# Self-attention scores as pairs of 64-row matmuls into two banks, and one input's statistics behind the softmax of a step

## The reference

```python
q = (xp @ Wq + bq)            # 16 heads of 32 features
k = (xp @ Wk + bk)            # 2 groups of 32 features
v = (xp @ Wv + bv)
starts = jnp.arange(num_windows) * (W // 2)      # W = 64
idx = starts[:, None] + jnp.arange(W)
scores = jnp.einsum('brgnqd,bgnkd->brgnqk', qg, kw) * scale
attn = jax.nn.softmax(scores, axis=-1)
og = jnp.einsum('brgnqk,bgnkd->brgnqd', attn, vw)
x = x + (o @ Wo + bo)
```

## Time and profile before

| what | value |
|---|---|
| median of 3 runs | 2509.7 us (2509.41 to 2511.34) |
| profiled execution | 2509.38 us |
| its span, first to last instruction | 2507.7 us |
| TensorE busy | 2419.8 us (96%) |
| weight loads busy | 2203.8 us (88%) |
| VectorE busy | 1680.1 us (67%) |
| ScalarE busy | 1302.3 us (52%) |
| GpSimd busy | 1169.9 us (47%) |
| windows 179 to 229 us, one turn | TensorE 48.81, VectorE 39.93, ScalarE 36.83, GpSimd 37.77 us busy, granted clock 1.00 |
| window 34 to 42 us, in turn 0 | TensorE 6.64 of 8.00 us busy, granted clock 0.79 |

### The profile page before, as it was taken

One profiled execution on the slowest core, in us unless ns is written; L12 is line 12 of the kernel. 1 busy time (PEld: TensorE's weight loads), 2 busy tenths in 40 slices (PEclk: granted clock), 3 DMA queues, 4 the chain that ended last, 5 costly groups with the idle time before them and its releaser, 6 DMA issues. The chain is left out here.

```text
span 2507.7 us, 45795 instructions
## 1 busy us (share of the span) xinstructions
PE 2419.8 (96%) x14893; PEld 2203.8 (88%) x14893; DVE 1680.1 (67%) x4774; ACT 1302.3 (52%) x3307; POOL 1169.9 (47%) x1561
## 2 busy tenths in 40 slices
PE   7999998899999999999999999999999999999798
PEld 6998998789989998999898889999999999999686
DVE  7877887566565756565666666675757575767676
ACT  6777776455454545454554545454545454545511
POOL 6767776344343435343433434343435353435254
PEclk9999999999999999999999999999999999999899
DMA  4445456211111211211222211111111111122343
GB/s 143 159 148 172 168 167 218 104 46 58 44 54 54 65 40 54 58 44 54 61 92 60 84 35 59 44 54 54 55 47 61 43 55 54 44 73 95 126 145 121
DMA packets 101476, 207.69 MB, mean 83 GB/s; under 512 B 20048, under 2 KB 49456, under 8 KB 101152
## 3 DMA queue, kind: packets, MB, share of 16 engines
q1 hardware_dynamic: 95680, 186.78, 23.2%
q0 software_dynamic: 5600, 18.41, 2.2%
HBM read 139.83 MB, written 65.32 MB: 82 GB/s over the span
## 5 line engine op out<-in xcount | busy, mean ns | idle before, releaser
L1436 POOL TENSOR_SCALAR x_probs<-x_probs,x_inv 112x376 f32<-112x376 f32 x512 | 634.6, 1250 | 190.7 <-DVE x_inv L1636 190.7
L1430 POOL TENSOR_SCALAR x_bias<-x_top 112x1 f32<-112x1 f32 x512 | 124.1, 242 | 878.4 <-DVE x_top L1608 878.0
L1492 ACT ACTIVATE x_probs<-x_probs,x_bias 112x376 f32<-112x376 f32 x512 | 308.4, 603 | 421.0 <-POOL x_bias L1430 421.0
L1751 PE MATMUL x_ps_r<-x_wo,x_oT 128*128 128x512 f32 x1344 | 344.4, 392 | 1.4 <-DVE x_wo L1534 1.4
L1697 PEld LDWEIGHTS x_ps_o<-x_pT,x_v 128*128 128x128 f32 (+1 forms) x2304 | 294.2, 191 | 35.9 <-DVE x_pT L1615 17.5
L1737 PE MATMUL x_ps_f<-x_xT,x_wq 128*128 128x448 f32 x1440 | 319.2, 371 | 2.6 <-DVE x_v L1579 2.0
L1697 PE MATMUL x_ps_s<-x_kT,x_qT 128*112 128x376 f32 x1536 | 311.6, 338 | 3.5 <-DVE x_top L1608 3.4
L1697 PE MATMUL x_ps_f<-x_wv,ctxT 128*128 128x512 f32 (+1 forms) x1152 | 305.7, 403 | 8.0 <-DVE x_kT L1579 4.8
L1697 PE MATMUL x_ps_o<-x_pT,x_v 128*128 128x224 f32 (+1 forms) x2304 | 299.3, 274 | 11.8 <-DVE x_pT L1615 11.7
L1697 PE MATMUL x_ps_f<-ctxT,x_wk 128*128 128x376 f32 x1512 | 300.3, 334 | 2.1 <-DVE x_kT L1579 2.1
L1737 PEld LDWEIGHTS x_ps_f<-x_xT,x_wq 128*128 128x128 f32 x1440 | 262.6, 188 | 28.7 <-DVE x_v L1579 8.7
(11 more groups left out here) (236 smaller groups left out, 4000.3 us busy)
## 6 DMA issues: line engine op xcount, KB each, us to landing
ctxT<-ctxs SPq DMA_DIRECT2D x62, 752.0 KB, 4.5
ctxs<-ctxT SPq DMA_DIRECT2D x32, 752.0 KB, 5.0
x_xT<-h2T SPq DMA_DIRECT2D x15, 896.0 KB, 4.9
room<-in_ctx_dram SPq DMA_DIRECT2D x32, 256.0 KB
experts<-in_L_ffn_W_dram SPq DMA_DIRECT2D x32, 256.0 KB, 4.6
w_xa<-in_x_dram SPq DMA_DIRECT2D x32, 224.0 KB, 4.7
w_xr<-in_x_dram SPq DMA_DIRECT2D x32, 224.0 KB, 4.2
x<-w_xr SPq DMA_DIRECT2D x32, 224.0 KB, 5.1
```

The costliest lines, as they stand in the source:

```text
L1430: pool.tensor_scalar(bias[:, m:m + 1], top[:, m:m + 1], -0.1 * NEG, -SCALE, ALU.max, ALU.mult) \
L1436: pool.tensor_scalar(probs[0:T, m, 0:SE], probs[0:T, m, 0:SE], inv[:, m:m + 1], None, ALU.mult).then_inc(normed, 1)
L1492: act.activation(probs[0:T, m, 0:SE], probs[0:T, m, 0:SE], ACT.Exp, bias=bias[:, m:m + 1], scale=SCALE, accum_out=total[:, m:m + 1]).then_ ...
L1751: last = pe.matmul(ps_r[:], oT[:, a, h, slot:slot + P], wo[:, b_, h, :], start=h == 0 and (a, b_) == PASSES[0], stop=h == H - 1 and (a, b_ ...
```

## The change

The scores of a chunk are computed by halves of the rows. For each of the six products of a chunk there are two matmuls, one with rows 0 to 63 and one with rows 64 to 127, and each has only the 128 columns of `kd` in which these rows have values. The lower half writes bank `ps_s[0]`, the upper half `ps_s[1]`. A step then has 48 matmuls of 64 rows by 112 by 128 columns in place of 24 of 128 rows by 112 by 256 columns. Both banks are complete at the end of the block. The heads of a bank come in another order, and the product with the values reads `pT` in that order.

There is one wait for the banks at the start of a block in place of one per bank, and in step 0 a wait per chunk for the Q fill in place of one per two chunks.

Input 2 of the next turn moves from early to late in step 1 (`AHEAD`): its statistics on VectorE stand between the two `totals`, its `factors1` on GpSimd behind `normalise`. ScalarE's `norm1` of it moves to step 2, ahead of `exps` (`NORM_NEXT`). This holds for turns 0 to 6.

```diff
-    AHEAD = [([0], [1]), ([2], []), ([3], []), ([], [])]
+    AHEAD = [([0], [1]), ([], [2]), ([3], []), ([], [])]
+    NORM_NEXT = {1: [2]}
...
+                    ahead = fills.which(turn) in ("first", "full")
+                    if ahead:
+                        for n in NORM_NEXT.get(s - 1, []):
+                            norm1(Turn(turn.at + 1, turn.reg), n)
                     if "S" in kinds:
                         exps(turn, s)
-                    early, late = AHEAD[s] if fills.which(turn) in ("first", "full") else ([], [])
+                    early, late = AHEAD[s] if ahead else ([], [])
+                    late = [n for n in late if n not in NORM_NEXT.get(s, [])]
...
-                                             pT[:, b_].rearrange("p (c q) t -> p q c t", q=2)[:, q, :, lo:hi])
+                                             pT[:, b_].rearrange("p (q c) t -> p q c t", q=2)[:, q, :, lo:hi])
...
                 def scores(turn, s):
-                    for u in range(2):
+                    if not (turn.reg is None and turn.at == 0 and s == 0):
+
+                        pe.wait_ge(less_ready, turn.count(8, 2 * s))
+                    jobs = [(w, q, a, b_) for w, q in enumerate((qa, qb)) for a, b_ in PASSES]
+                    for m in range(KC):
                         if s == 0:
-                            pe.wait_ge(fill_done, fills.until(turn.before(), ("Q", 2 * u + 1)))
-                        if not (turn.reg is None and turn.at == 0 and s == 0):
-
-                            pe.wait_ge(less_ready, turn.count(8, 2 * s + u - 1))
-                        for m in range(2 * u, 2 * u + 2):
-                            last = product(ps_s[u][0:T, (m % 2) * 4 * WIN:(m % 2 + 1) * 4 * WIN],
-                                           [(q[:, a, m, s, :], kd[:, b_, s, w, :])
-                                            for w, q in enumerate((qa, qb)) for a, b_ in PASSES])
-                        last.then_inc(scores_ready, 1)
+                            pe.wait_ge(fill_done, fills.until(turn.before(), ("Q", m)))
+                        for n, (w, q, a, b_) in enumerate(jobs):
+                            for u in range(2):
+                                rows = slice(2 * D * u, 2 * D * (u + 1))
+                                last = pe.matmul(ps_s[u][0:T, m * 2 * WIN:(m + 1) * 2 * WIN], q[rows, a, m, s, :],
+                                                 kd[rows, b_, s, w, 2 * WIN * u:2 * WIN * (u + 1)],
+                                                 start=n == 0, stop=n == len(jobs) - 1)
+                                if m == KC - 1 and n == len(jobs) - 1:
+                                    last.then_inc(scores_ready, 1)
```

## The result

The changed kernel takes 2519.3 us (median of 6, 2517.2 to 2524.9), the one before 2509.6 us (6, 2509.3 to 2511.3): a ratio of 1.0041, 95% interval 1.0031 to 1.0051. It is slower, by 0.41%. The prediction said slower, 2516 in 2504 to 2574. The profiled execution took 2519.57 us with a span of 2517.9 (before 2509.38 and 2507.7), so some 10.2 us are to be explained.

What follows compares the result with a forecast made beforehand. TensorE's own work was taken to bound steps 3 and 0, GpSimd's queue step 2. Turns 1 to 6 +5.0, turn 0 +2.1 less 0.3, turn 7 -0.3 or nothing: +6.5 on 2509.4 gives 2516 us, range 2504 to 2574.

Steps and rivals of the forecast that it cites:

- The pairs' price: TensorE's score block: 0.098 us a pair plus 0.31 for changing row modes, gaining 0.15 us in steps 0 and 3.
- Rival 1: Score block: the two halves' loads run one after the other, +2.0 us per TensorE-bound step, 2572 us in all; chance 0.20.
- Rival 2: Score block: loads overlap, matmuls or issue don't quite, 0.107 to 0.14 us a pair, 2528 us in all; chance 0.10.
- Rival 4: Score block: a pair costs no more than 0.062 us, block 1.8 us, 2500 us in all; chance 0.14.
- The banks: VectorE's maxima: both banks complete only at the block's end; no cost in steady turns, a cost in turn 0.
- The statistics: Steps 1 and 2: moved `factors1` lengthens GpSimd's line, step 3's scores start 1.13 us later, TensorE waits for `pT`.
- Rival 3: Step 2: the wait put down to ScalarE's copy is the true bound, not GpSimd; 2507 us in all; chance 0.10.
- Turns 1 to 6 in all: Steady turns: +1.13 less twice 0.15 makes +0.83 us a turn, six times +5.0.
- Turn 0: First turn: +2.1 us from later maxima and the statistics behind them, less 0.3.
- The late maxima: Turn 0, step 1: VectorE's maxima start 1.5 us later, at about 40.5 instead of 38.96, waiting for both banks.
- a fall of the clock: Steady turns: prediction counted as wrong if the granted clock, 1.00 there, falls with half-row matmuls.
- Turn 7: Last turn: takes no statistics, so -0.3 us or nothing.

Runs made afterwards that it cites:

- e4: Changed kernel with each of the 48 score matmuls on all 128 rows and 128 columns, in the same order: 2577.6 us, ratio 1.026.
- e3: Changed kernel with all 24 lower-half matmuls first, then all 24 upper-half ones, so no pairs: 2614.6 us, ratio 1.040.
- e1: Changed kernel with input 2's statistics back in their old place, so the pairs alone: 2514.9 us, ratio 1.0009 to the kernel before.
- e2: Changed kernel with the old 24 matmuls and old order of heads, so the moved statistics alone: 2519.3 us, ratio 1.0023 to the kernel before.
- e7: Changed kernel with GpSimd's output bias addition cut to 8 of 512 columns: 2512.0 us, ratio 1.0007 to the kernel before.
- e5: Changed kernel with the old whole-row matmuls in turn 0 only, pairs in turns 1 to 7: 2517.8 us, ratio 1.0027 to the kernel before.
- e8: Changed kernel with whole rows in turn 0 and input 2's statistics in their old place: 2510.6 us, ratio 1.0001 to the kernel before.
- e9: Changed kernel with turn 7's splits of both `x_wk` and `x_xT` moved behind step 3's softmax: 2521.8 us, ratio 1.0036 to the kernel before.
- e6: Changed kernel with only turn 7's split of `x_xT` moved behind step 3's softmax: 2517.6 us, ratio 1.0033 to the kernel before.

## Why the prediction was right, and where its size was off

The direction and the mechanism in the steady turns held; the sum was short by 3.7 of 10.2 us, in the first and the last turn.

- **The pairs' price.** Forecast 0.098 us a pair and a gain of 0.15 us in steps 0 and 3; measured 0.098, and 0.13 and 0.19. The block takes 2.50 us, 0.39 less than before, of which 0.13 to 0.19 reach the step. The rest is the change between whole and half rows, and the rows give it: 0.86 instead of 0.70 us ahead of the first score, 0.11 us behind the block, and 0.15 within it (2.50 against 24 x 0.098 = 2.35). That is 0.42 in all where I had put 0.31, and it is the full rows (e4), at 0.70 again, that tie the first part to the half rows. Rivals 1, 2 and 4 fall: single halves in e3 cost 0.098 each, pairs no more. The block was to be 2.7 to 2.8 us from first score to next kind; it is 2.50, since part of the price of the change lies outside of it.
- **The banks.** In the steady turns the maxima begin later and nothing waits, as forecast: e1 keeps step 1 at 10.75 us and step 2 at 10.05.
- **The statistics.** Forecast +1.13 us for steps 1 and 2 together; measured 10.19+11.62-10.75-10.08 = +0.98. The waits came where they were forecast: 0.74 for `pT` (about 1 was said), then before the transposes. The normalisations end 11.6 us apart, the number forecast. e2 has the loss without the pairs, and e7 gives back 1.07 us for 1.09 off the bias. Rival 3 falls. The reading behind it, that "a wait put down to ScalarE" hid GpSimd, is borne out, since after the change the same waits carry GpSimd's name.
- **Turns 1 to 6 in all.** Forecast +5.0, measured +3.8: 0.83 a turn was 0.19 too much, for the statistics' term was 0.15 too large.
- **Turn 0, the mis-sized term.** Forecast +1.8, measured +3.3. The late maxima were right in kind, and larger: they begin 2.4 us later (41.34, was 38.96; 1.5 was said), 0.4 of it because the block itself starts later (36.77, was 36.34), and the value product starts 48.33-45.76 = 2.6 us later. What was left out is a change of the clock. I had listed a fall of the clock as something that would make the prediction wrong, but had looked only at turns where it was 1.00. For turn 0 (0.79 in its window) I noted that part of the block ran at half clock, and then gave the changed kernel no more of it than the kernel before. With pairs it stays at half for 17.1 us instead of 6.8; the value product's 2.84 instead of 1.87 us is 1.0 of it. With whole rows in turn 0 (e5) the half clock is 6.8 us again and the turn 1.8 us shorter. How the 3.3 us divide between the late banks, the moved statistics (0.8 by e2) and the clock is known only to about 1 us, as e8 shows.
- **Turn 7, the step that failed.** Forecast -0.3 "or nothing", measured +2.6. "Turn 7 takes no statistics" looked only at what is moved, and not at what its later GpSimd work would meet: the splits of the next stage on VectorE, which exist in this turn alone. e9 shows the cause by taking them away (4.64 to 0.37 us) and e6 by making another operation slow. Why GpSimd is later there has two parts, by its low part of the context against the scores of step 3: -0.4 us before and -0.3 in e2, +1.0 in e1, +2.2 after, -0.2 in e7. The timelines give the rest of the way. In step 2 of turn 7 VectorE waits for the scores in both kernels, and with pairs its first maxima begin 2.6 us after the block's start instead of 1.6; that is the late bank, which I had priced at nothing outside turn 0. GpSimd's normalisation, which waits for VectorE's reciprocals there, comes 0.9 us later by the same measure (6.3 instead of 5.4), in e1 as in the changed kernel. Step 3's scores in turn come 0.4 us earlier. With the move GpSimd is 0.2 us later still, measured from these scores: the last operation of GpSimd's chain starts 0.14 us ahead of `x_wk` in e1 and 0.07 behind it in the changed kernel, and is then held for 1.0 us. The size of this step was read and not tried by itself.

Turn 0 gave 1.5 us more than forecast and turn 7 2.9, the steady turns 1.2 less: hence a time 3 us over the forecast, with the direction unharmed. That the steady turns were forecast too high is luck for the sum: it hides 1.2 of the 4.4 us that were missed.

## What to carry to other kernels

Cost a change in the loop's steady turn, and then walk through the first and the last turn with their own rows: more than half of what this one lost lay in 2 turns of 8. Look for what only these turns hold, such as a throttled clock or the next stage's preparation. Work that fills an engine's pause is free only where that engine isn't the bound of the next step; moved behind, it stands in the line that sets the end. When TensorE's own time shrinks in a loop that another engine bounds, the gain is the few tenths of the steps that it bounds.

## What the runs showed of the hardware

- A matmul with 128 moving columns and 112 stationary ones costs 0.098 us with 64 rows as with 128, and two with different halves of the rows cost 0.098 together. What makes a pair worth anything is that they alternate: in order, the block takes 4.5 us instead of 2.50.
- Going from 128 rows to 64 cost 0.16 us (0.86 instead of 0.70 us from the transposes to the first score), coming back 0.11 us. The gain of a block of pairs, 0.39 us, shrank by this to 0.13 to 0.19 in the step.
- The granted clock differed at the same busy share. From 37 to 41 us the changed kernel's TensorE was busy 4.00 of 4.00 us at a granted clock of 0.51; the whole-row matmuls of the kernel before, also 4.00 of 4.00, had 0.61 there and came back to full in 3.4 us. Halves in order brought it down to 0.90 over 100 us at 99% busy. What the chip goes by, these rows don't tell: the full rows with 128 columns (e4) kept 1.00 in steady turns, yet had 34 us at half in turn 0. Executions differ in how long it lasts (13.7 to 23.9 us with pairs), and their times go with it: the changed kernel's six run from 2517.2 us at a mean clock of 0.990 to 2524.9 at 0.986. Only the profiled execution tells where in the span the half clock lay.
- In turns 0 and 7 of the kernels before and after, each fall of the clock came during a pause of TensorE of 1.9 to 4.6 us or within 2 us behind it, and the clock then stayed at half through stretches in which the engine was busy all the time.
- A two-input operation of VectorE took 5.67 and 5.08 us instead of 2.03 and 1.23, since GpSimd's low part had started up to 0.27 us earlier. It isn't a slowing in proportion: they ended 1.9 and 1.1 us after GpSimd's second low part of `pT`, about what they take alone. It isn't always held through several of GpSimd's operations: in e1 `x_xT`, started 0.34 us behind the first of the two low parts of `pT`, took 2.98 us and got in between them, and the second then took 2.91 us instead of about 1.1. What decides that, these rows don't tell.
